# One-hots made in halves of two fields on ScalarE, ten instead of eight

## The reference

```python
e = jnp.stack([tbl_0[ids[:, 0]], ..., tbl_39[ids[:, 39]]], axis=1)   # 512 x 40 x 32
xi, xj = e[:, iidx, :], e[:, jidx, :]                                # the 780 pairs
z = jnp.einsum('bpd,pde,bpe->bp', xi, bilinear_matrices, xj)
h = jnp.concatenate([z, dense_ctx], axis=1)
h = jnp.maximum(h @ W_top1 + b_top1, 0.0)
h = jnp.maximum(h @ W_top2 + b_top2, 0.0)
y = h @ W_top3
```

## Time and profile before

| | |
|---|---|
| median of 3 runs | 189.72 us (189.65 to 190.01) |
| the profiled execution | 189.45 us, its span 187.6 us |
| PE, share of the span | 93% |
| DVE | 79% |
| ACT | 28% |
| POOL | 56% |

### The profile page before, as it was taken

The page is one execution under the profiler, slowest core; times in us unless marked ns, Lnnn a source line. Parts: engine busy times, 40 slices in busy tenths (PEclk is TensorE's granted clock), DMA queues, the critical chain, the costliest instruction groups (busy, mean ns, idle before and its releaser), DMA issues.

```text
span 187.6 us, 4092 instructions
## 1 busy us (share of the span) xinstructions
PE 174.1 (93%) x1766; PEld 59.9 (32%) x1766; DVE 148.9 (79%) x147; ACT 52.9 (28%) x52; POOL 105.8 (56%) x114
## 2 busy tenths in 40 slices
PE   6789788889999999999999999799999997998992
PEld 6434323233332233232323323223323242332340
DVE  1898999989599899899899999768899985770502
ACT  3875596898100201112110111102110111111501
POOL 2687777877877777777777777778600022202000
PEclk9969999999999999999999999999999999999999
DMA  5996130341055970220000010000000000000000
GB/s 153 350 410 254 17 98 14 108 124 19 14 153 102 330 285 14 73 106 18 13 15 14 14 17 11 14 18 12 3 0 0 3 0 0 5 0 0 3 0 0
DMA packets 7786, 13.07 MB, mean 70 GB/s; under 512 B 2164, under 2 KB 4728, under 8 KB 7768
## 3 DMA queue, kind: packets, MB, share of 16 engines
q1 hardware_dynamic: 4552, 11.15, 17.2%
q0 software_dynamic: 3072, 1.58, 4.8%
q10 hardware_dynamic: 144, 0.08, 0.3%
HBM read 12.67 MB, written 0.00 MB: 68 GB/s over the span
## 4 chain that ended last, share of the span: by engine, by line
PE 84%; ACT 8%; DVE 3%; DMA 2%; issue 2%; DVEq 0%; ACTq 0%
PE ps_t L679 27%; PE ps_z L693 27%; PE ps_x L727 9%; PE ps_x L642 7%; PE ps_t L738 4%; PE ps_t L673 3%; ACT hot_act L508 3%; ACT hot_act L510 3%; DMA ids<-ids_oh 2%; PE ps_t L713 2%; PE ps_x L654 2%; PE ps_z L642 1%; PE ps_t L706 1%; DVE hot_dve L556 1%; PE ps_t L642 1%
## 5 line engine op out<-in xcount | busy, mean ns | idle before, releaser
L596 DVE TENSOR_TENSOR prod<-ps_t,xt 128x1024 f32<-128x1024 f32 x100 | 116.7, 1218 | 18.3 <-PE ps_t L679 15.6
L485 POOL DMA_INDIRECT emb<-tbl,idx x96 | 94.5, 985 | 32.8 <-issue 29.0
L679 PE MATMUL ps_t<-xt,w_sb 32*128 32x512 f32 x360 | 54.3, 640 | 0.0
L693 PE MATMUL ps_z<-prod,ones 128*32 128x512 f32 x400 | 53.3, 605 | 0.0
L493 POOL TENSOR_TENSOR late_z<-late_z,tbl_oh 128x512 f32<-128x512 f32 x8 | 10.2, 1289 | 30.6 <-ACT tbl_oh L537 30.6
L727 PE MATMUL ps_x<-late_z,late_w 128*32 128x256 f32 x320 | 22.6, 379 | 2.0 <-ACT tbl_oh L537 2.0
L679 PEld LDWEIGHTS ps_t<-xt,w_sb 32*128 32x128 f32 x360 | 16.6, 183 | 22.5 <-issue 15.0
L556 DVE TENSOR_SCALAR hot_dve<-ids,ramp 128x2048 bf16<-128x2048 int16 x26 | 18.6, 763 | 3.7 <-DMA ids<-ids_oh 3.7
L693 PEld LDWEIGHTS ps_z<-prod,ones 128*32 128x32 f32 x400 | 7.9, 108 | 38.2 <-DVE prod L596 22.1
L727 PEld LDWEIGHTS ps_x<-late_z,late_w 128*32 128x32 f32 x320 | 10.3, 110 | 20.9 <-issue 19.0
L508 ACT ACTIVATE hot_act<-ids,neg_ramp 128x2048 bf16<-128x2048 int16 x8 | 15.9, 1992 | 2.7 <-DMA ids<-ids_oh 2.7
(11 more groups left out here) (64 smaller groups left out, 92.1 us busy)
## 6 DMA issues: line engine op xcount, KB each, us to landing
ids<-ids_oh SPq DMA_DIRECT2D x4, 512.0 KB, 7.0
emb<-tbl,idx POOLq DMA_INDIRECT x96, 2.3
late_w<-w SPq DMA_DIRECT2D x1, 1280.0 KB, 8.4
tbl_oh<-small_tables SPq DMA_DIRECT2D x2, 512.0 KB, 8.0
w_sb<-w_pairs SPq DMA_DIRECT2D x1, 704.0 KB
tbl_oh<-small_tables SPq DMA_DIRECT2D x1, 640.0 KB, 11.3
w_sb<-w_pairs SPq DMA_DIRECT2D x1, 640.0 KB
w_sb<-w_pairs SPq DMA_DIRECT2D x1, 576.0 KB, 4.5
```

What stands on the lines that cost most here:

```text
L485: nc.gpsimd.indirect_dma_start(emb[:, n % E_RING, t, u * D:(u + 1) * D], None, tables[field], bass.IndirectOffsetOnAxis(ap=idx[:, at:at + ...
L596: nc.vector.tensor_tensor(prod[:, g % PROD_RING, :].rearrange("p (i b) -> p i b", i=2), ps_t[PAIR[g]][:, :].rearrange("p (i b) -> p i b", ...
L679: last = nc.tensor.matmul(o, w_sb[s * D:(s + 1) * D, at:at + P], xt[s * D:(s + 1) * D, kk, :], start=True, stop=True)
L693: last = nc.tensor.matmul(ps_z[q * D:(q + 1) * D, :], ones[:, v * D:(v + 1) * D], prod[:, t // 2 % PROD_RING, t % 2 * B:(t % 2 + 1) * B], ...
```

## The change

ACT makes a one-hot in two halves of two fields, 1024 elements each, with an Abs and a Relu for each half. Between its moves it now counts in halves: five before the loop, then 3, 4, 2 and 6 after the moves of block 0, 1, 2 and 3. It makes ten one-hots instead of eight: in block 1, (1,3) and (1,6) in place of (1,5), and in block 4 also (3,9). DVE makes 24 instead of 26; (1,5) is now its own. ACT's ring has three places instead of two. PE waits for both halves of a one-hot before it takes it.

```diff
-ON_ACT = [(0, 3), (0, 6), (1, 5), (2, 3), (2, 6), (3, 1), (3, 4), (3, 7)]
-
-ACT_MAKES_FIRST, ACT_MAKES_AFTER = 2, {0: 1, 1: 2, 2: 1, 3: 2}
-assert len(ON_ACT) == ACT_MAKES_FIRST + sum(ACT_MAKES_AFTER.values())
+ON_ACT = [(0, 3), (0, 6), (1, 3), (1, 6), (2, 3), (2, 6), (3, 1), (3, 4), (3, 7), (3, 9)]
+
+ACT_MAKES_FIRST, ACT_MAKES_AFTER = 5, {0: 3, 1: 4, 2: 2, 3: 6}
+assert 2 * len(ON_ACT) == ACT_MAKES_FIRST + sum(ACT_MAKES_AFTER.values())
...
-E_RING, PROD_RING, DVE_RING, ACT_RING = 4, 6, 4, 2
+E_RING, PROD_RING, DVE_RING, ACT_RING = 4, 6, 4, 3
...
-            def one_hot(n):
+            def one_hot(n, half):
 
                 j, c = ACT_HOTS[n]
-                if n == 0 or ACT_HOTS[n - 1][0] != j:
-                    act.wait_ge(ids_oh_in[j], 16)
-                wait_slot(act, ACT_HOTS, n, ACT_RING, hot_used_act)
-                o = hot_act[:, n % ACT_RING, :, :]
+                if half == 0:
+                    if n == 0 or ACT_HOTS[n - 1][0] != j:
+                        act.wait_ge(ids_oh_in[j], 16)
+                    wait_slot(act, ACT_HOTS, n, ACT_RING, hot_used_act)
+                fields = slice(half * FB // 2, (half + 1) * FB // 2)
+                o = hot_act[:, n % ACT_RING, fields, :]
                 at = OH_FIRST[j] + c
-                nc.scalar.activation(o, ids_oh[:, j, :, :], ACT.Abs, bias=neg_ramp[:, at:at + 1]).then_inc(distance_made, 1)
-                act.wait_ge(distance_made, n + 1)
+                nc.scalar.activation(o, ids_oh[:, j, fields, :], ACT.Abs,
+                                     bias=neg_ramp[:, at:at + 1]).then_inc(distance_made, 1)
+                act.wait_ge(distance_made, 2 * n + half + 1)
                 nc.scalar.activation(o, o, ACT.Relu, bias=1.0, scale=-1.0).then_inc(hot_made_act, 1)
...
             for _ in range(ACT_MAKES_FIRST):
-                one_hot(act_hots)
+                one_hot(act_hots // 2, act_hots % 2)
                 act_hots += 1
...
                     for _ in range(ACT_MAKES_AFTER.get(k, 0)):
-                        one_hot(act_hots)
+                        one_hot(act_hots // 2, act_hots % 2)
                         act_hots += 1
...
-                    pe.wait_ge(made, n + 1)
+                    pe.wait_ge(made, 2 * (n + 1) if k in ACT_HOTS else n + 1)
```

## The result

The changed kernel takes 194.34 us in the median of six executions (193.75 to 195.10), the kernel before 189.80 in six on the same chip; the ratio is 1.0247, with a 95% interval of 1.023 to 1.0264. The forecast was 194.2 us. The profiled execution took 194.46 us, its span is 192.7.

The account below looks back on a forecast made before the run. PE and DVE bound the kernel after 63.2 us, so time lost earlier, in the one-hot part paced by ACT, reaches the end: late (3,9), 54.34 - 49.88 = 4.46 us, on 189.72 gives 194.2 us, range 192.6 to 195.8.

Parts of the forecast that it names:

- The price of a half: On ACT, a half one-hot takes 2.14 us, so 4.29 per one-hot instead of 3.85.
- the chain through ACT: Late halves delay ACT's moves and PE behind them: block 1's move 1.91 us late, block 2's 2.79.
- The stalls at (1,6), (2,3) and (3,9): PE waits for ACT's halves in blocks 1, 2 and 4: 2.2, 2.0 and another 1.67 us.
- the wait before (2,0): PE's old 1.70 us wait for DVE's one-hot before (2,0) only changes place, to (1,6).
- (3,9) alone: Late stall in block 4's one-hots: ready at 54.34, PE there at 52.67, another 1.67 us.
- DVE's relief: One one-hot fewer, 0.70 us, ahead of (2,0), ready at 23.7 instead of 24.36; rival that it decides (faster): 0.05.
- Part 1: Before the loop: five halves end at 16.06, block 0's move is due at 16.05; cost 0.01, taken as nothing.
- No wait of PE on a DMA or on POOL to swallow it: In the loop after the one-hots nothing is early, so all 4.46 us of delay stay.
- the rival "absorbed": PE or DVE is ahead of something undelayed later, so the stalls vanish: no change, 189.7 us; chance 0.03.
- The clock: Rival: PE's clock falls in a new stall, adding 0 to 1.3 us, middle 0.7, so 194.9; chance 0.27.
- The upper end of the sum: If 1024 elements cost two activations of 512, a half takes 2.55 us and the whole loss is +9.8 us.
- h: ACT's time per half one-hot, taken as 2.14 us, between 1.93 and 2.55; the loss is 13h - 23.36.

Follow-up runs that it names:

- Quarters: The kernel before with its eight ACT one-hots each made in four parts of one field (512 elements): 195.63 us, ratio 1.031.
- the kernel with filled stalls: The changed kernel with seven 128-column identity matmuls on PE ahead of its waits for (1,6) and (2,3): 193.77 us, ratio 1.0216 to the kernel before.
- the ten whole one-hots: The changed kernel with ACT's ten one-hots made whole instead of in halves: 191.85 us, ratio 1.0097 to the kernel before.
- the eight in halves: The kernel before with its eight ACT one-hots in halves and three places: 190.40 us, ratio 1.0013; with two gathers left out 190.26 us.
- the kernel with two places: The changed kernel with two places for ACT's one-hots instead of three: 193.88 us, ratio 1.0229 to the kernel before.
- the version with (2,0) on ACT: Against the kernel before: nine ACT one-hots, whole but (1,5), with (2,0), (2,4), (2,7) replacing (2,3), (2,6): 189.91 us; two gathers out 188.32.
- the two versions nearest to it: Nine ACT one-hots including (2,0), only (1,5) in halves: 189.91 us; the kernel before with (1,5) alone in halves and three places: 190.12 us.

## Why the prediction was right, and what in it was not

**The price of a half, and the chain through ACT: right.** 2.14 us forecast and measured. The stalls at (1,6), (2,3) and (3,9), the wait before (2,0) that goes, and the moves that carry the delay on are in the trace at the places named. (3,9) alone was sized at 1.67 and came to 1.67. The changed kernel at full clock takes (3,9) at 54.18, where 54.34 was forecast. Quarters came out at 5.5 us for 5.7, but by the same errors that cancel, told below, and are no proof of the size.

**DVE's relief: right.** It only moved the old wait; (2,0) at 24.66 against 24.36 in the earlier trace rows, and at full clock, in the kernel with filled stalls, at 24.33 against 23.94.

**The starting point, Part 1: wrong by half a us.** The forecast had the five halves cost nothing, because block 0 was moved at 16.05 in the earlier trace rows; it named the condition, ACT's idle stretch, and did not ask whether that stretch was usual. The execution had PE at half clock from 10.3 to 13.6. With its clock kept the kernel before moves block 0 at 14.9, DVE does not wait for group 0, PE takes (2,0) at 23.94 instead of 24.36 and (3,9) at 49.23 instead of 49.88. The halves hold the changed one at 16.0 in either case, and PE, which at full clock comes sooner than the earlier trace rows show, idles 1.0 us for (0,6) too. The cost on the path of the one-hots is 193.69 - 188.65 = 5.0 us by time and 54.18 - 49.23 = 4.95 by the traces, not 4.46.

**"No wait of PE on a DMA or on POOL to swallow it": wrong by 1.1 us.** The kernel before gains that much when two gathers are left out, and the changed one nothing. The trace that I read shows no such wait, but its 64th gather had landed only about 1.2 us before PE came, in an execution where the gathers were early, and the prediction did not look how far ahead they were. I had put the rival "absorbed" as all or nothing, and it came in part: 193.69 - 189.75 = 3.9 us is what the change costs at full clock (193.78 against 189.80 on the first chip: 4.0). The same two corrections bring the two misses among the experiments near: the ten whole one-hots have (3,9) 52.33 - 49.23 = 3.1 us late, less 1.1 is 2.0, and 1.7 was measured; the eight in halves cost 1.6, less 1.1 is 0.5, and 0.3 was measured.

**The clock: under full in four of six executions.** Priced at 0 to 1.3 us and 0.7 in the middle; those executions took 0.4 to 1.3 us more, and lift the median from 193.8 to 194.3. In the profiled execution it fell after the stall at (2,3), not at (1,6) as the rival had it, and made PE last at (2,6) by half a us. The traces of the kernel with two places and of the changed kernel with two gathers out show it after (1,6).

**The upper end of the sum was too low.** At h = 2.55 the five halves of Part 1 would end at 18.1, 2.0 us behind the move they were to be covered by, and that is not in the +9.8. It did not matter, since h came out at 2.14.

So the forecast of 4.46 stands beside a measured 4.54 that is made of other parts: 5.0 on the path, 1.1 taken back, 0.5 with the fallen clocks (4.4; the remaining 0.1 is within the spread of the runs). The first two are differences to the same kernel with two gathers out, so that they add up to the 3.9 by themselves. The sign and the mechanism were right; that the size fits this well is luck, two errors and a rival that cancel.

Whether a version with ten one-hots could beat the kernel before was not found; the version with (2,0) on ACT shortens the one-hot part, and cannot show it while block 7 is gathered as late as it is.

## What to carry to other kernels

Before handing work to an engine with a low busy share, follow it in order of time: ACT was busy for 28% of the span before the change, and after it last in the part that counted, and a cut into halves there costs its fixed price at each part. A gap that is idle in one profiled execution may be made by that execution's clock; look for a stretch below full clock ahead of it before counting on it as cover. And ask of a stage that is to be shortened which producer that runs on its own, as POOL's gathers do, arrives just ahead of it or just behind, and by how much: here that producer stood 1.2 us ahead in one trace, and waits of 1.0 and 1.1 us stood in two others. Gains vanish there, and losses are partly forgiven, so that equal steps up and down do not cost the same.

## What the runs showed of the hardware

PE's clock after idling is a matter of the execution. After 1.78 us of idling before 10.3 to 10.6 us it fell in the trace of the kernel before and in that of the changed kernel with two places, and stayed at full in the changed kernel's. After the 2.13 us of idling before (1,6) it fell in the kernel with two places and in the changed kernel with two gathers out, and stayed at full in the changed kernel and with (3,9) on DVE. After the 1.88 us before (2,3) it fell in the changed kernel and stayed with (3,9) on DVE. With matmuls of an identity in both idle times the mean clock was at 0.997 or more in five of five executions; 8 of 17 executions of the unfilled forms (the changed kernel, with two places, with two gathers out) were at 0.991 or less, on three chips, so this may be chance.

The distance from one gather of POOL to the next, 128 rows each, was 1.24 to 1.26 us from 50 us on in every trace (one of 1.33 in the quarters' apart), and 1.24 to 2.07 us before. The start of the 64th differed by 1.9 us between the traces of the kernel before and of the two versions nearest to it (88.24, 89.30, 90.12).
